# A graph network on one core: the place one-hots of the sort batches, and their products with the code, made in two halves of 64 places with a stop behind the first

## The chip, the core and the metric

The kernel runs on 1 core of one Trainium2 chip. The metric is the time on the device, in microseconds (us), of one execution; the number given for a kernel is the median of its runs. A profile is taken of one execution of its own, whose time stands beside the others.

## What is computed

Two graph layers over 3125 nodes of 128 features and 50,000 edges, the first a sum of neighbours with a small network behind it, the second a sum of messages whose weight depends on the edge's type (16 types, made of 8 bases):

```python
h = jnp.maximum(_layernorm(x, axis=-1), 0.0)
neigh = jax.ops.segment_sum(h[src], dst, num_segments=3125)
rst = (1.0 + eps[0]) * h + neigh
x = x + relu(relu(rst @ W1 + b1) @ W2 + b2)
h = jnp.maximum(_layernorm(x, axis=-1), 0.0)
weights = jnp.einsum('rb,bio->rio', coefficients, bases)
out = h @ w_self.T
msg = h[dst] @ weights[edge_type_16]      # per edge: one of 16 matrices
x = x + out.at[src].add(msg)
```

## The kernel before

**Sorting edges by matmul.** The edges are put into chunks of 128 that share a bucket of target nodes, so that a chunk's sum is a matrix product. There are four sorts, numbered 0 to 3: sorts 0, 1 and 2 take 72, 128 and 200 columns of 125 edges of the first layer and give 77, 131 and 208 chunks; sort 3 (`LAST`) takes all 400 columns of the second layer and gives 410 chunks. A sort places each edge's code at (place 0 to 127, chunk) in PSUM bank 7: VectorE makes a one-hot of the place and a one-hot of the chunk, one of the two is multiplied by the code, and TensorE multiplies them. Columns go in batches of 8 (`BATCH`), and the operands of a batch have two buffers (`BATCH_BUFS`). So sort 1 has 16 batches, sort 2 has 25 and sort 3 has 50.

**One batch of sort 3** (`sort_batch`): VectorE waits until TensorE has used the buffer (`batch_used`), makes the place one-hots of 8 columns in one instruction, `place_hot` of 125 x 1024 (L733), stops for it (`place_ready`), makes `place_val_a`, its product with the code's high part, in one instruction of the same size (L738), stops for it, and makes 8 chunk one-hots of 410 (L743). ScalarE starts at `place_ready` and makes 8 products with the code's low part, `place_val_b` (L498). TensorE then runs 16 products of 410 columns (L972, L974). **One batch of sorts 1 and 2** (`sort_pair`): one `place_hot` (L752), a stop, and 8 chunk one-hots already multiplied by the code's high part (L758); ScalarE adds the low part (L490); TensorE runs 8 products (L982).

**Gathering and adding up beside the next sort.** While sort s+1 is made, the chunks of sort s are added up (`groups_beside`): in groups of 4 chunks for the first layer, VectorE makes a `node_hot` for each chunk (L806), GpSimd gathers the chunk's 128 rows of the table `h_table` by an indirect DMA (L423), and TensorE multiplies the gathered rows by the node_hot (L1003, 3 products a chunk). Beside sort 3 run 47 of the 52 groups of sort 2; its last 5 come behind the decoding of sort 3 (`groups_rest`). Each engine has its own program, and the order within one is as written:

```python
for g in range(BESIDE[s + 1][1]):
    group_work(s, g)

    batches_alone(s + 1, sort_batch, *batches_after(s + 1, g))
```

**How far GpSimd may run ahead.** The first layer has 105 groups in all (20, 33 and 52, here numbered 0 to 104 across the three sorts), whose rows go round a ring of 13 groups. Before GpSimd gathers group g it waits until TensorE has used group g - lag:

```python
left = GROUPS_L[0] - gg if l == 0 else 2 * RING_L[1] - (gg - RING_L[1])
return min(RING_L[l], max(LEAST_LAG + l, left // 2))
```

The lag is 13 up to group 79, falls by one every two groups from there, and is 4 from group 96. Behind the first layer's last group come the dense part, the storing of the second layer's table and the gathers of the second layer. The helper `own` makes VectorE wait for the end of the instruction it was given, by semaphore `v`. Behind each `sort_batch` and `sort_pair` the same engine goes on with the next group's node_hots.

Of the kernel before, what the change touches and what calls it, by code (L numbers as in the profile page):

```python
# [9 lines left out]
ALU = mybir.AluOpType  # L10
# [4 lines left out]
P = 128  # L15
# [8 lines left out]
EP = N_EDGES // EC  # L24
# [33 lines left out]
BATCH = 8  # L58
# [21 lines left out]
def build(nc, x, src, dst, etype, eps, W1, b1, W2, b2, bases, coef, w_self, out):  # L80
    ctx = ExitStack()
    with ctx:
        def sb(name, shape, dt):
            return ctx.enter_context(nc.sbuf_tensor(name, shape, dt))
# [13 lines left out]
        iota_run = sb("iota_run", [P, P, BATCH], F16)  # L98
# [41 lines left out]
        place_h = [sb(f"place_h{l}", [EP, EC], F16) for l in range(2)]  # L140
        code_a = [sb(f"code_a{l}", [EP, EC], F16) for l in range(2)]
# [16 lines left out]
        place_hot = sb("place_hot", [EP, BATCH_BUFS, P, BATCH], F16)  # L158
        place_val_a = sb("place_val_a", [EP, BATCH_BUFS, P, BATCH], F16)
# [390 lines left out]
        def _(dve):  # L550
            done = 0

            def own(ins):

                nonlocal done
                ins.then_inc(v, 1)
                done += 1
                dve.wait_ge(v, done)

            V = nc.vector  # L560
# [167 lines left out]
            def sort_batch(s, batch, buf):  # L728

                l, c0, *_ = SORTS[s]  # L730
                dve.wait_ge(batch_used, batch + (BATCHES_BEFORE[s] + 1))
                run = slice(c0 + batch * BATCH, c0 + (batch + 1) * BATCH)
                V.tensor_tensor(place_hot[:, buf, :, :], iota_run[0:EP, :, :],  # L733
                                place_h[l][:, run].rearrange("p (o c) -> p o c", o=1).to_broadcast([EP, P, BATCH]),
                                ALU.is_equal).then_inc(place_ready, 1)
                done_before = batch + (BATCHES_BEFORE[s] - BATCHES_BEFORE[1] + 1)
                dve.wait_ge(place_ready, done_before)
                V.tensor_tensor(place_val_a[:, buf, :, :], place_hot[:, buf, :, :],  # L738
                                code_a[l][:, run].rearrange("p (o c) -> p o c", o=1).to_broadcast([EP, P, BATCH]),
                                ALU.mult).then_inc(val_a_ready, 1)  # L740
                dve.wait_ge(val_a_ready, batch + 1)
                for i in range(BATCH):
                    last = V.tensor_scalar(chunk_hot[:, buf, i, 0:CHUNKS[s]], iota_h[0:EP, 0:CHUNKS[s]],  # L743
                                           chunk_f[l][:, c0 + batch * BATCH + i:c0 + batch * BATCH + i + 1], None, ALU.is_equal)
                last.then_inc(batch_ready, 1)

            def sort_pair(s, batch, buf):

                l, c0, *_ = SORTS[s]
                dve.wait_ge(batch_used, batch + (BATCHES_BEFORE[s] + 1))  # L750
                run = slice(c0 + batch * BATCH, c0 + (batch + 1) * BATCH)
                V.tensor_tensor(place_hot[:, buf, :, :], iota_run[0:EP, :, :],  # L752
                                place_h[l][:, run].rearrange("p (o c) -> p o c", o=1).to_broadcast([EP, P, BATCH]),
                                ALU.is_equal).then_inc(place_ready, 1)
                dve.wait_ge(place_ready, batch + (BATCHES_BEFORE[s] - BATCHES_BEFORE[1] + 1))
                for i in range(BATCH):
                    c = c0 + batch * BATCH + i
                    V.tensor_scalar(pair_hot_of[s][:, buf, i, 0, :], iota_h[0:EP, 0:CHUNKS[s]], chunk_f[l][:, c:c + 1],  # L758
                                    code_f[:, c:c + 1], ALU.is_equal, ALU.mult).then_inc(pair_ready, 1)
# [99 lines left out]
            for s in range(1, NSORT):  # L859

                rank_place(s)
                if s > 1:

                    dve.wait_ge(nhot_used, CHUNKS_BEFORE[s - 1])
                groups_beside(s - 1, node_hots, sort_batch if s == LAST else sort_pair)
                if s == LAST:
                    read_sorted(s)
                else:
                    read_pair(s)
                decode(s)  # L870
                groups_rest(s - 1, node_hots)
                if s < LAST:
                    if s + 1 == LAST:
                        dve.wait_ge(w_stored, 32)
                    rank_count(s + 1)
# [248 lines left out]
```

## Time and profile before

| | |
|---|---|
| time, median of 3 runs | 1236.69 us (1233.98 to 1239.51) |
| time of the profiled execution | 1234.93 us |
| its span, first to last instruction | 1233.1 us |
| VectorE busy | 718.0 us (58%) |
| TensorE busy | 897.0 us (73%) |
| GpSimd busy | 834.9 us (68%) |
| ScalarE busy | 372.5 us (30%) |
| 416 gathers of the first layer, busy | 443.7 us |
| 410 gathers of the second layer, busy | 388.6 us |

The shares are means over stages that differ: sort 3 runs from about 409 to 616 us, the first layer's last product ends at 642 us, and the second layer's gathers fill the time from 772 us on. An engine's idle time matters only where another one waits for it, so the table is to be read with the rows of each stage. Times within the profile count from the start of the span.

### The profile page before, as it was taken

The numbers are of one execution on the slowest core, as the hardware profiler recorded it, in microseconds if no ns is written. First come the engines' busy times: TensorE is split into PE (matmuls) and PEld (weight loads), VectorE is DVE, ScalarE is ACT, GpSimd is POOL, SyncE is SP. The second block draws the span as 40 slices with busy tenths as digits, with TensorE's granted clock in tenths as the row PEclk, the third lists the DMA queues.
The fourth block names the chain that finished last, engine by engine and source line by source line (L and its number), as shares of the span: only waits on it lengthen the run. The fifth ranks groups of instructions, "written<-read, shape, count | busy, mean of one in ns | idle before, by whom it ended". The sixth has DMA issues, their size and how long they took to land.

```text
span 1233.1 us, 13150 instructions
## 1 busy us (share of the span) xinstructions
PE 897.0 (73%) x3799; PEld 571.9 (46%) x3799; DVE 718.0 (58%) x2165; ACT 372.5 (30%) x945; POOL 834.9 (68%) x833
## 2 busy tenths in 40 slices
PE   4777848978744899999959998965655655655654
PEld 2443424434312577777634433844444444444443
DVE  7896569857578899999935432833222323322331
ACT  7444314635300588888804432000000000000001
POOL 0177757778777777777740475777777777777772
PEclk9688878989986899999968999977777777677677
DMA  4443323433342334334333898212122122121224
GB/s 100 121 134 113 108 61 101 135 105 100 107 110 75 106 105 133 110 105 138 107 49 121 264 299 266 54 52 54 52 54 54 51 54 53 52 53 52 53 54 73
DMA packets 50307, 122.86 MB, mean 100 GB/s; under 512 B 16156, under 2 KB 27021, under 8 KB 47487
## 3 DMA queue, kind: packets, MB, share of 16 engines
q0 software_dynamic: 33088, 67.82, 21.8%
q1 hardware_dynamic: 16844, 52.62, 13.5%
q10 hardware_dynamic: 308, 1.60, 0.5%
q8 instruction: 34, 0.56, 0.2%
q14 instruction: 33, 0.27, 0.1%
HBM read 71.86 MB, written 50.10 MB: 99 GB/s over the span
## 4 chain that ended last, share of the span: by engine, by line
POOL 25%; issue 9%; PE 8%; SPq 4%; DVE 2%; DMA 2%; ACT 0%; POOLq 0%; DVEq 0%; ACTq 0%
POOL gathered L423 25%; SPq L382 4%; PE ps L999 3%; PE ps L1081 2%; DMA gathered<-z_table,row_of 1%; DVE spare L890 1%; PE ps L1058 1%; PE ps L1048 1%; PE ps L1095 0%; DMA z_table<-spare 0%; DMA gathered<-h_table,row_of 0%; PE ps L1003 0%; DVE x_sb L920 0%; ACT spare L519 0%; DVE stats L580 0%
## 5 line engine op out<-in xcount | busy, mean ns | idle before, releaser
L423 POOL DMA_INDIRECT gathered<-h_table,row_of x416 | 443.7, 1067 | 187.7 <-issue 120.1
L423 POOL DMA_INDIRECT gathered<-z_table,row_of x410 | 388.6, 948 | 190.4 <-issue 120.0
L999 PE MATMUL ps<-node_hot,gathered 128*128 128x250 f32 x820 | 279.7, 511 | 170.7 <-DMA gathered<-z_table,row_of 170.7
L806 DVE TENSOR_SCALAR node_hot<-iota_f,key_of 128x250 f32<-128x250 f32 x410 | 153.8, 379 | 294.3 <-PE ps L999 286.1
L999 PEld LDWEIGHTS ps<-node_hot,gathered 128*128 128x128 f32 x820 | 208.1, 262 | 242.1 <-issue 207.0
L1003 PE MATMUL ps<-node_hot,gathered 128*128 128x506 bf16 (+1 forms) x1248 | 243.8, 350 | 75.9 <-DMA gathered<-h_table,row_of 57.6
L1003 PEld LDWEIGHTS ps<-node_hot,gathered 128*128 128x128 bf16 x1248 | 126.5, 103 | 179.4 <-issue 112.1
L498 ACT ACTIVATE place_val_b<-place_hot,code_b 125x128 f16<-125x128 f16 x400 | 173.8, 520 | 100.5 <-DVE place_hot L733 100.3
L490 ACT ACTIVATE scratch<-scratch,code_b 125x208 f16<-125x208 f16 (+1 forms) x328 | 114.4, 430 | 177.3 <-DVE scratch L758 177.3
L545 ACT COPY spare<-ps 128x500 f32<-128x500 f32 (+1 forms) x7 | 3.1, 563 | 459.8 <-PE ps L999 459.8
L972 PE MATMUL ps<-scratch,place_val_a 125*128 125x410 f16 x400 | 138.3, 346 | 2.6 <-DVE scratch L743 2.4
L974 PE MATMUL ps<-scratch,place_val_b 125*128 125x410 f16 x400 | 134.9, 337 | 0.0
L806 DVE TENSOR_SCALAR node_hot<-iota_h,key_of 128x506 bf16<-128x506 f16 (+1 forms) x416 | 107.5, 323 | 28.9 <-PE ps L1003 28.4
L743 DVE TENSOR_SCALAR scratch<-iota_h,chunk_f 125x410 f16<-125x410 f16 x400 | 102.6, 331 | 1.8
L1081 PE MATMUL ps<-w_rel,spare 128*125 128x512 f32 x200 | 90.7, 601 | 4.1 <-DVE spare L890 2.3
L758 DVE TENSOR_SCALAR scratch<-iota_h,chunk_f,spot_i 125x208 f16<-125x208 f16 (+1 forms) x328 | 83.7, 350 | 1.5
L972 PEld LDWEIGHTS ps<-scratch,place_val_a 125*128 125x128 f16 x400 | 57.6, 144 | 37.5 <-DVE scratch L743 6.7
L890 DVE COPY spare<-ps 125x1024 f32<-125x1024 f32 x25 | 30.5, 1221 | 60.1 <-PE ps L1081 32.4
L1081 PEld LDWEIGHTS ps<-w_rel,spare 128*125 128x125 f32 x200 | 35.5, 187 | 55.4 <-issue 31.7
L982 PE MATMUL ps<-scratch,place_hot 125*128 125x416 f16 (+1 forms) x328 | 57.1, 316 | 0.0
L982 PEld LDWEIGHTS ps<-scratch,place_hot 125*128 125x128 f16 x328 | 44.7, 145 | 14.0 <-issue 2.2
L752 DVE TENSOR_TENSOR place_hot<-iota_run,place_h 125x1024 f16<-125x1024 f16 x41 | 28.3, 689 | 39.1 <-PE ps L982 38.7
(170 smaller groups left out, 541.8 us busy)
## 6 DMA issues: line engine op xcount, KB each, us to landing
z_table<-spare SPq DMA_DIRECT2D x50, 448.0 KB
z_table<-zeros_z SPq DMA_DIRECT2D x19, 896.0 KB
gathered<-h_table,row_of POOLq DMA_INDIRECT x416
gathered<-z_table,row_of POOLq DMA_INDIRECT x410, 2.5
z_table<-spare SPq DMA_DIRECT2D x50, 52.0 KB
z_table<-zeros_z SPq DMA_DIRECT2D x19, 104.0 KB
out<-x_sb SPq DMA_DIRECT2D x6, 224.0 KB
h_table<-gathered SPq DMA_DIRECT2D x1, 1092.0 KB
```

The lines of the kernel that those rows point to most:

```text
L423: pool.indirect_dma_start(place if s == LAST else place.rearrange("p j d -> p (j d)"), None, z_table if s == LAST else h_table, bass.Indir ...
L490: nc.scalar.activation(pair_hot_of[s][:, buf, i, 1, :], pair_hot_of[s][:, buf, i, 0, :], ACT.Copy, scale=code_b[l][:, c0 + batch * BATCH + ...
L498: nc.scalar.activation(place_val_b[:, buf, i, :], place_hot[:, buf, :, i], ACT.Copy, scale=code_b[l][:, c0 + batch * BATCH + i:c0 + batch ...
L743: last = V.tensor_scalar(chunk_hot[:, buf, i, 0:CHUNKS[s]], iota_h[0:EP, 0:CHUNKS[s]], chunk_f[l][:, c0 + batch * BATCH + i:c0 + batch * B ...
L758: V.tensor_scalar(pair_hot_of[s][:, buf, i, 0, :], iota_h[0:EP, 0:CHUNKS[s]], chunk_f[l][:, c:c + 1], code_f[:, c:c + 1], ALU.is_equal, AL ...
L806: V.tensor_scalar(node_hot_of[s][:, k % HOTS[s], :], (iota_f if s == LAST else iota_h)[:, 0:WIDE[s]], key_of[s][:, k:k + 1], None, ALU.is_ ...
L972: T.matmul(ps[:, 7, 0:w], place_val_a[:, buf, :, i], hot, start=False, stop=False, skip_group_check=True)
L974: last = T.matmul(ps[:, 7, 0:w], place_val_b[:, buf, i, :], hot, start=False, stop=False, skip_group_check=True)
L982: last = T.matmul(ps[:, 7, 0:2 * CHUNKS[s]].rearrange("p (k w) -> p k w", k=2), place_hot[:, buf, :, i], pair_hot_of[s][:, buf, i, :, :], ...
L999: last = T.matmul(psf[:, bass.ds(offs[i], WIDE[s])], rows, node_hot_of[s][:, k % HOTS[s], :], start=False, stop=False, skip_group_check=True)
L1003: last = T.matmul(psf[:, bass.ds(offs[i], WIDE[s])], rows[:, part, :], node_hot_of[s][:, k % HOTS[s], :], start=False, stop=False, skip_gr ...
L1081: last = T.matmul(z_half(half)[:, q * BANK:(q + 1) * BANK], h2T[:, t * NP:(t + 1) * NP], w_rel[:, half * N_REL // 2 + q * BT:half * N_REL ...
```

## The change

In `sort_batch` and `sort_pair` the instruction that makes the place one-hots is made in two of 64 places, 125 x 512 each, and VectorE waits for the first before it issues the second; in `sort_batch` the same is done with their product with the code. What is computed is the same. Sort 0 (`sort_first`) is as before, and no other engine's program changes.

```diff
                 run = slice(c0 + batch * BATCH, c0 + (batch + 1) * BATCH)
-                V.tensor_tensor(place_hot[:, buf, :, :], iota_run[0:EP, :, :],
-                                place_h[l][:, run].rearrange("p (o c) -> p o c", o=1).to_broadcast([EP, P, BATCH]),
+                half = P // 2
+                places = place_h[l][:, run].rearrange("p (o c) -> p o c", o=1).to_broadcast([EP, half, BATCH])
+                own(V.tensor_tensor(place_hot[:, buf, 0:half, :], iota_run[0:EP, 0:half, :], places, ALU.is_equal))
+                V.tensor_tensor(place_hot[:, buf, half:P, :], iota_run[0:EP, half:P, :], places,
                                 ALU.is_equal).then_inc(place_ready, 1)
                 done_before = batch + (BATCHES_BEFORE[s] - BATCHES_BEFORE[1] + 1)
                 dve.wait_ge(place_ready, done_before)
-                V.tensor_tensor(place_val_a[:, buf, :, :], place_hot[:, buf, :, :],
-                                code_a[l][:, run].rearrange("p (o c) -> p o c", o=1).to_broadcast([EP, P, BATCH]),
+                codes = code_a[l][:, run].rearrange("p (o c) -> p o c", o=1).to_broadcast([EP, half, BATCH])
+                own(V.tensor_tensor(place_val_a[:, buf, 0:half, :], place_hot[:, buf, 0:half, :], codes, ALU.mult))
+                V.tensor_tensor(place_val_a[:, buf, half:P, :], place_hot[:, buf, half:P, :], codes,
                                 ALU.mult).then_inc(val_a_ready, 1)
                 dve.wait_ge(val_a_ready, batch + 1)
...
```

The second hunk makes the same edit to `place_hot` in `sort_pair`.

On VectorE, in the middle of sort 3, one batch and the group behind it stood like this before (`scratch` holds the chunk one-hots there):

```order
L733 TENSOR_TENSOR place_hot<-iota_run,place_h 125x1024 [waits batch_used]
L738 TENSOR_TENSOR place_val_a<-place_hot,code_a 125x1024 [waits place_ready]
L743 TENSOR_SCALAR scratch<-iota_h,chunk_f 125x410 [waits val_a_ready]
L743 TENSOR_SCALAR scratch<-iota_h,chunk_f 125x410 x7
L806 TENSOR_SCALAR node_hot<-iota_h,key_of 128x250 x4
```

At the same place of VectorE's program there now stand:

```order
L735 TENSOR_TENSOR place_hot<-iota_run,place_h 125x512 [waits batch_used]
L736 TENSOR_TENSOR place_hot<-iota_run,place_h 125x512 [waits v]
L741 TENSOR_TENSOR place_val_a<-place_hot,code_a 125x512 [waits place_ready]
L742 TENSOR_TENSOR place_val_a<-place_hot,code_a 125x512 [waits v]
L746 TENSOR_SCALAR scratch<-iota_h,chunk_f 125x410 [waits val_a_ready]
L746 TENSOR_SCALAR scratch<-iota_h,chunk_f 125x410 x7
L811 TENSOR_SCALAR node_hot<-iota_h,key_of 128x250 x4
```

Nothing changed places; two instructions and two waits for VectorE's own semaphore came in, and the lines below are numbered 3 or 5 higher.

On VectorE, in the middle of sort 2, a batch and its group stood like this before (`scratch` holds the chunk one-hots times the code):

```order
L752 TENSOR_TENSOR place_hot<-iota_run,place_h 125x1024 [waits batch_used]
L758 TENSOR_SCALAR scratch<-iota_h,chunk_f,spot_i 125x208 [waits place_ready]
L758 TENSOR_SCALAR scratch<-iota_h,chunk_f,spot_i 125x208 x7
L806 TENSOR_SCALAR node_hot<-iota_h,key_of 128x506 [waits nhot_used] x4
L752 TENSOR_TENSOR place_hot<-iota_run,place_h 125x1024 [waits batch_used]
```

and stand now:

```order
L757 TENSOR_TENSOR place_hot<-iota_run,place_h 125x512 [waits batch_used]
L758 TENSOR_TENSOR place_hot<-iota_run,place_h 125x512 [waits v]
L763 TENSOR_SCALAR scratch<-iota_h,chunk_f,spot_i 125x208 [waits place_ready]
L763 TENSOR_SCALAR scratch<-iota_h,chunk_f,spot_i 125x208 x7
L811 TENSOR_SCALAR node_hot<-iota_h,key_of 128x506 [waits nhot_used] x8
```

Here one instruction and one wait came in a batch.

## Rows read from the trace of the kernel before

**Rows 1.** Busy time by stage: us, busy (count) by engine, TensorE's clock, DMA share, GB/s

```profile
409.00:470.00 61.00, 59.56 (x385) 42.63 (x386) 59.99 (x201) 48.91 (x113) 47.84 (x44) 0.94 0.42 121
470.00:530.00 60.00, 59.61 (x401) 43.03 (x398) 58.99 (x202) 51.23 (x119) 46.89 (x44) 1.00 0.38 106
530.00:616.00 86.00, 85.06 (x568) 61.23 (x566) 84.29 (x287) 73.34 (x170) 67.11 (x63) 1.00 0.42 120
```

**Rows 2.** Groups by shape, 409 to 616 us: count | busy us, mean ns | idle before

```profile
L423 POOL DMA_INDIRECT gathered<-h_table,row_of x149 | 162.7, 1092 | 45.4 <-issue 41.8 <-PE ps L1003 3.7
L743 DVE TENSOR_SCALAR scratch<-iota_h,chunk_f 125x410 f16<-125x410 f16 x400 | 102.6, 331 | 1.8
L738 DVE TENSOR_TENSOR place_val_a<-place_hot,code_a 125x1024 f16<-125x1024 f16 x50 | 34.6, 692 | 1.7
L733 DVE TENSOR_TENSOR place_hot<-iota_run,place_h 125x1024 f16<-125x1024 f16 x50 | 33.9, 679 | 0.0
```

**Rows 3.** Timeline of VectorE in sort 3: start us, us

```profile
480.90 0.68 DVE L733 TENSOR_TENSOR place_hot<-iota_run,place_h 125x1024 f16<-125x1024 f16 x1
481.62 0.69 DVE L738 TENSOR_TENSOR place_val_a<-place_hot,code_a 125x1024 f16<-125x1024 f16 x1
482.35 1.99 DVE L743 TENSOR_SCALAR scratch<-iota_h,chunk_f 125x410 f16<-125x410 f16 x8
485.02 0.68 DVE L733 TENSOR_TENSOR place_hot<-iota_run,place_h 125x1024 f16<-125x1024 f16 x1
```

**Rows 4.** Timeline of TensorE in sort 3: first and last product of a batch, a group

```profile
484.40 0.39 PE L972 MATMUL ps<-scratch,place_val_a 125*128 125x410 f16 x1
487.07 0.33 PE L974 MATMUL ps<-scratch,place_val_b 125*128 125x410 f16 x1
487.24 1.45 PE L1003 MATMUL ps<-node_hot,gathered 128*128 128x250 bf16 x12
```

**Rows 5.** Timeline of VectorE in sort 0, whose instructions stand close

```profile
29.08 0.69 DVE L723 TENSOR_TENSOR place_hot<-iota_run,place_h 125x1024 f16<-125x1024 f16 x1 [0.26 <-PE ps L962]
29.69 0.47 DVE L724 TENSOR_TENSOR scratch<-iota_run,chunk_h 125x616 f16<-125x616 f16 x1
30.59 0.47 DVE L726 TENSOR_TENSOR scratch<-scratch,first_b 125x616 f16<-125x616 f16 x1
30.98 0.22 DVE L824 RECIPROCAL rstd<-sd 125x12 f32<-125x12 f32 x1
```

**Rows 6.** Waits of the whole span: us in total, times, longest

```profile
DVE place_hot L752 <- PE ps L982: 38.7, 16, 6.3
PE ps L1003 <- DMA gathered<-h_table,row_of: 57.6, 22, 5.5
```

**Rows 7.** Timeline of GpSimd: a gather beside L738, one alone, one beside L733

```profile
469.85 1.42 POOL L423 DMA_INDIRECT gathered<-h_table,row_of  x1 [0.30 <-issue]
471.57 0.95 POOL L423 DMA_INDIRECT gathered<-h_table,row_of  x1 [0.30 <-issue]
481.33 1.08 POOL L423 DMA_INDIRECT gathered<-h_table,row_of  x1 [0.30 <-issue]
```

**Rows 8.** Timeline: TensorE's use of group 92, GpSimd's first gather of group 96

```profile
581.65 1.45 PE L1003 MATMUL ps<-node_hot,gathered 128*128 128x250 bf16 x12
586.73 1.10 POOL L423 DMA_INDIRECT gathered<-h_table,row_of  x1 [0.30 <-PE ps L1003]
```

**Rows 9.** Timeline of the end of the first layer

```profile
622.27 6.66 PE L1003 MATMUL ps<-node_hot,gathered 128*128 128x250 bf16 x36 [3.45 <-DVE node_hot L806]
629.98 0.95 POOL L423 DMA_INDIRECT gathered<-h_table,row_of  x1 [0.30 <-issue]
633.73 0.95 POOL L423 DMA_INDIRECT gathered<-h_table,row_of  x1 [0.30 <-issue]
639.51 2.68 PE L1003 MATMUL ps<-node_hot,gathered 128*128 128x250 bf16 x12 [4.17 <-DMA gathered<-h_table,row_of]
642.22 3.02 DVE L881 COPY scratch<-ps 128x500 f32<-128x500 f32 x5 [16.60 <-PE ps L1003]
```

More of the change, by code:

```diff
@@ L751, in sort_pair @@
                 run = slice(c0 + batch * BATCH, c0 + (batch + 1) * BATCH)
-                V.tensor_tensor(place_hot[:, buf, :, :], iota_run[0:EP, :, :],
-                                place_h[l][:, run].rearrange("p (o c) -> p o c", o=1).to_broadcast([EP, P, BATCH]),
+                half = P // 2
+                places = place_h[l][:, run].rearrange("p (o c) -> p o c", o=1).to_broadcast([EP, half, BATCH])
+                own(V.tensor_tensor(place_hot[:, buf, 0:half, :], iota_run[0:EP, 0:half, :], places, ALU.is_equal))
+                V.tensor_tensor(place_hot[:, buf, half:P, :], iota_run[0:EP, half:P, :], places,
                                 ALU.is_equal).then_inc(place_ready, 1)
```

## The prediction

> **What bounds the kernel now.** I read the busy time by stage first. From 409 to 616 us, while sort 3 is made, VectorE is busy for 203.3 of 207 us and TensorE for 204.2 [rows 1], so the mean of 58% for VectorE over the span says nothing about this stretch. The reader should see that three engines are full there at once: GpSimd too, since 149 gathers of 1.092 us with 0.30 us between them make 207 us [rows 2, 7]. So the question is which of the three has to wait for another.
>
> The groups of that stage answer for VectorE. Before `place_hot`, the instruction that waits for TensorE to free a buffer, VectorE sat idle for 0.0 us in 50 batches, and before the other two kinds for 1.7 and 1.8 us in all [rows 2]. It never waits, so sort 3 runs at VectorE's pace. The timeline gives that pace: from one `place_hot` to the next 485.02 - 480.90 = 4.12 us, group of node_hots included [rows 3]. TensorE needs almost as much: 487.24 - 484.40 = 2.84 us for the 16 products and at most 1.45 us for the group's 12, so at most 4.29 us and by its timeline about 4.1 [rows 4].
>
> GpSimd needs 4 x (1.092 + 0.30) = 5.6 us for a group of four, more than the 4.12 us in which a group is used. It starts the stage with up to 13 groups gathered and lives on them. By group 96 it has 586.73 - (581.65 + 1.45) = 3.6 us between TensorE's use of group 92 and its own start [rows 8]. At the end it is late: TensorE waits 4.17 us for the last group's rows, and the first layer's sums are copied out at 642.22 us [rows 9]. So the end of the first layer is set by GpSimd by a small margin, with VectorE right behind it.
>
> In sorts 1 and 2 it is otherwise: VectorE waits 38.7 us for TensorE before `place_hot`, and TensorE waits 57.6 us for gathers of the first layer [rows 6]. There GpSimd sets the pace and VectorE has time to spare.
>
> **The cost of one split.** Without a stop, VectorE's next instruction starts 29.69 - 29.08 = 0.61 us behind a place one-hot of 1024, and 30.98 - 30.59 = 0.39 us behind one of 616 [rows 5]. That is 0.22 us for 408 elements, 0.54 ns each, so 512 elements are worth 0.275 us and the rest of an instruction is about 0.06 us. With a stop the same 1024 take 0.72 and 0.73 us from start to start [rows 3]. A half with a stop is then 0.725 - 0.275 = 0.45 us, two halves 0.90, and a split costs 0.175 us; since these rows are rounded to 0.01 us I take 0.18. It can't be under 0.06, which an instruction costs with no stop at all. From above, the smallest instruction here with a stop behind it bounds it: the reciprocal of 12 elements takes 0.22 us [rows 5], so with a gap of 0.03 us at most 0.25.
>
> **Where it is hidden.** Sorts 1 and 2 have 16 + 25 = 41 splits, 7.4 us of VectorE. They lie in the 38.7 us in which VectorE waits for TensorE before just this instruction [rows 6], so I cost them at nothing; without that cover they would cost the 7.4 us.
>
> **Where it is not.** Sort 3 has 50 batches with two splits each: 100 x 0.18 = 18.0 us, on an engine with no idle time in that stage. The period with a group goes from 4.12 to 4.48 us, and TensorE's 4.1 to 4.29 us still fits, so VectorE stays the bound. Behind the waiting instruction stand the chunk one-hots and the next group's node_hots, for which TensorE waits, and TensorE's use of a group is what GpSimd waits for. ScalarE gets its place one-hots 0.18 us later in each batch; its 8 products take 48.91 + 51.23 + 73.34 = 173.5 of the 207 us [rows 1], so it is no new bound.
>
> **What comes back to GpSimd.** A gather beside the two long instructions took 1.42 us, one beside a place one-hot 1.08 us, one alone 0.95 us [rows 7]. So these VectorE instructions hold a gather up, and halves with a stop between them should hold it up less. Before sort 3 this counts, because GpSimd sets the pace there: with 41 place one-hots, a stretch of 0.13 us and half of it saved, at most 2.7 us, at least nothing, since not each meets a gather. I take 1.5 us: sort 3 starts that much earlier. In sort 3 what GpSimd gains turns into waiting. The use of group 92 comes 42 batches into the sort, so 42 x 0.36 - 1.5 = 13.6 us later, and the 3.6 us [rows 8] are used up: GpSimd must wait for it, and group 96 starts at about 597 instead of 586.7 us.
>
> The Trainium skill, "SBUF — State Buffer", section "Who interferes with whom", says that a tensor_tensor with both inputs in SBUF takes only the read side of the port pair that VectorE and GpSimd share, and infers that generating a DMA's descriptors is not held up by it. The 1.42 us of rows 7 speak against the inference. By the page the 1.5 us would not come back and the sum would be 12 instead of 10.5 us.
>
> **The end of the layer.** The sorted columns are ready for the last five groups 18.0 - 1.5 = 16.5 us later. Group 100 is the first of the 36 products that start at 622.27 us and take 6.66 us [rows 9]; it is used by about 624.9 us, as the first of the three at the lowered clock. GpSimd's gathers of group 104, the last, start at 629.98 us [rows 9] and need group 100 used: 5.1 us to spare. So they start 16.5 - 5.1 = 11.4 us later. Then 4 gathers of 1.25 us, the landing, and 2.68 us of products as before. The landing was slow: the last issue ended at 634.68 and TensorE began at 639.51 us, 4.8 us later [rows 9]. With group 103 issued before and then a pause, less stands in the DMA queues, which may give back between 0 and 3 us. I take 0.9.
>
> **Sum.** +18.0 - 1.5 - 5.1 - 0.9 = +10.5 us at the copy that stood at 642.22 us. What follows is unchanged and moves with it. The profiled execution took 1234.9 us (span 1233.1), 1.8 us under the median of 1236.7; against that median the changed kernel comes to 1247 us, 0.85% slower.
>
> **Rivals.**
>
> *Slower, by the page* (chance 0.05): GpSimd's descriptors are not held up by these instructions, and nothing comes back before sort 3: 1248.7 us. The row of 1.42 us is against it.
>
> *A stop costs little, or the end absorbs more* (0.15): at a split of 0.06 to 0.12 us, 100 splits are 6 to 12 us, and after 1.5 and 5.1 us of slack -0.6 to +5.4 are left; about 1239 us, no measurable change. For it: VectorE's start-to-start times are read from rounded rows. Against it: 0.72 against 0.61 us for the same 1024 elements is what a stop adds, 0.11 us, and the fixed 0.06 stands beside it.
>
> *Faster: GpSimd keeps the pace* (0.07). In sort 3, gathers lose 149 x (1.092 - 0.95) = 21 us [rows 2, 7]. If the halves return some 8 us of it and VectorE's added time stays within the slack, the last group is gathered that much earlier: 1229 us. It decides where a split costs VectorE under 0.05 us, so that 100 of them stay under the 5.1 us at the end. For it speaks that TensorE waits for gathers 57.6 us in all [rows 6]; against it, that VectorE has no idle time in just this stage.
>
> *Much slower: TensorE loses its full clock* (0.08). The granted clock in sort 3 was 0.94, 1.00 and 1.00 with TensorE busy 98% and more [rows 1]; the changed kernel has it wait some 0.2 to 0.4 us in each batch. Below a mean of 4.12 / 4.48 = 0.92 TensorE would be slower than VectorE; at 0.85 a batch takes 4.85 us, 0.37 us more, 18 us in all: 1265 us.
>
> **How the numbers follow.** The forecast has the remaining 0.65. Its own range is a split of 0.15 to 0.21 us (15 to 21 us), 0 to 2.7 us back, and 0 to 3 us at the landing: +4 to +16, with the ends rarely together, so 1242 to 1253. For 8 in 10 I add the flat case and part of the slow one: 1238 to 1258. The measurement can tell about 0.5%, 6.2 us. Faster is 0.07, within it is 0.15, and slower is the forecast, the page's case and the clock's: 0.78.
>
> **What would show it.** Right: in the profile after, the halves last about 0.42 us each, 100 of each kind of `place_hot` and `place_val_a` in sort 3; that stage's period is near 4.48 us; VectorE still has no idle time in it; a gather of the first layer is under 1.067 us in the mean; GpSimd's waits on `nhot_used` appear as gaps of several us from about group 90 on; the copy of 642.22 us stands near 653. Wrong: a period near 4.2, or TensorE at a granted clock under 0.95 between 415 and 630 us, or GpSimd without gaps.

## The result, and the profile after

| | before | after |
|---|---|---|
| time, median of 3 runs | 1236.69 us | 1247.64 us (1245.78 to 1248.31) |
| time of the profiled execution | 1234.93 us | 1245.78 us |
| its span | 1233.1 us | 1244.0 us |

The ratio is 1.0085, with a 95% interval of [1.0045, 1.0125]: the change made the kernel slower by 5.6 to 15.5 us. All comparisons in this document are of fast runs: one execution, of e6_after_lag13, took 2062 us and is left out.

The busy time of the changed kernel by stage, to be read against [rows 1] (us, busy and count of TensorE, its weight loads, VectorE, ScalarE, GpSimd, then TensorE's clock, DMA share, GB/s):

```profile
407.00:468.00 61.00, 56.82 (x359) 39.48 (x358) 59.13 (x211) 45.81 (x106) 46.98 (x47) 0.94 0.41 118
468.00:528.00 60.00, 55.55 (x361) 38.88 (x360) 58.16 (x209) 46.04 (x108) 41.66 (x43) 1.00 0.40 114
528.00:630.00 102.00, 93.77 (x612) 65.77 (x610) 98.95 (x351) 76.64 (x178) 61.00 (x63) 1.00 0.35 100
```

VectorE is busy for nearly as large a share as before, 97% after 98%; TensorE no longer: 206.1 of 223 us instead of 204.2 of 207. GpSimd fell too. TensorE's clock did not: 0.94, 1.00 and 1.00, as before. So one engine is full where three were.

The groups of sort 3 of the changed kernel, for [rows 2]:

```profile
L423 POOL DMA_INDIRECT gathered<-h_table,row_of x154 | 153.4, 996 | 74.6 <-issue 43.3 <-PE ps L1008 31.3
L977 PE MATMUL ps<-scratch,place_val_a 125*128 125x410 f16 x392 | 136.0, 347 | 17.2 <-DVE scratch L746 17.2
L746 DVE TENSOR_SCALAR scratch<-iota_h,chunk_f 125x410 f16<-125x410 f16 x399 | 104.7, 336 | 1.8
L742 DVE TENSOR_TENSOR place_val_a<-place_hot,code_a 125x512 f16<-125x512 f16 x50 | 21.3, 425 | 1.7
L736 DVE TENSOR_TENSOR place_hot<-iota_run,place_h 125x512 f16<-125x512 f16 x50 | 21.2, 425 | 1.7
L735 DVE TENSOR_TENSOR place_hot<-iota_run,place_h 125x512 f16<-125x512 f16 x49 | 20.2, 412 | 0.0
```

Four things are to be seen. A half lasts 412 to 425 ns, where the whole lasted 679 and 692: two halves are 0.15 us more, before the stop. VectorE still has no idle time before the instruction that waits for TensorE (L735). TensorE now waits 17.2 us for chunk one-hots. And GpSimd, whose gathers became shorter (996 instead of 1092 ns), now spends 31.3 us waiting for TensorE.

The timeline of VectorE in one batch, for [rows 3]:

```profile
483.74 0.41 DVE L735 TENSOR_TENSOR place_hot<-iota_run,place_h 125x512 f16<-125x512 f16 x1
484.19 0.42 DVE L736 TENSOR_TENSOR place_hot<-iota_run,place_h 125x512 f16<-125x512 f16 x1
484.65 0.42 DVE L741 TENSOR_TENSOR place_val_a<-place_hot,code_a 125x512 f16<-125x512 f16 x1
485.11 0.43 DVE L742 TENSOR_TENSOR place_val_a<-place_hot,code_a 125x512 f16<-125x512 f16 x1
485.57 2.13 DVE L746 TENSOR_SCALAR scratch<-iota_h,chunk_f 125x410 f16<-125x410 f16 x8
488.39 0.41 DVE L735 TENSOR_TENSOR place_hot<-iota_run,place_h 125x512 f16<-125x512 f16 x1
```

From the first half to the chunk one-hots are 485.57 - 483.74 = 1.83 us; before they were 482.35 - 480.90 = 1.45 [rows 3]. That is 0.38 us a batch, 0.19 a split. The period of this batch is 4.65 us instead of 4.12; the other 0.15 us lie in its chunk one-hots (2.13 us, where [rows 3] have 1.99) and behind. Over all 50 batches the mean is 228.1 / 50 = 4.56 us instead of 206.3 / 50 = 4.13.

GpSimd's timeline, where it now waits (for [rows 8]: the waits of 4 us have taken the place of the time to spare):

```profile
593.35 0.95 POOL L423 DMA_INDIRECT gathered<-h_table,row_of  x1 [0.30 <-issue]
598.27 0.97 POOL L423 DMA_INDIRECT gathered<-h_table,row_of  x1 [3.98 <-PE ps L1008]
```

The end of the first layer, for [rows 9]:

```profile
640.31 4.07 DVE L811 TENSOR_SCALAR node_hot<-iota_h,key_of 128x250 bf16<-128x250 f16 x20
640.83 5.31 PE L1008 MATMUL ps<-node_hot,gathered 128*128 128x250 bf16 x48 [3.25 <-DVE node_hot L811]
642.56 1.06 POOL L423 DMA_INDIRECT gathered<-h_table,row_of  x1 [3.13 <-PE ps L1008]
646.43 0.95 POOL L423 DMA_INDIRECT gathered<-h_table,row_of  x1 [0.30 <-issue]
651.33 2.68 PE L1008 MATMUL ps<-node_hot,gathered 128*128 128x250 bf16 x12 [5.18 <-DMA gathered<-h_table,row_of]
654.05 3.80 DVE L886 COPY scratch<-ps 128x500 f32<-128x500 f32 x7 [9.67 <-PE ps L1008]
```

The last gathers start as soon as TensorE has used group 100, after a wait of 3.13 us; before, they started without one. The copy of the sums moved from 642.22 to 654.05 us, by 11.8, and the span by 10.9.

### The profile page after: what moved, and what is told of

Same layout as the page of the kernel before. It is cut to its first block, busy times and chain, and to the rows that moved or that the text cites. A ratio compares the mean times of both kernels' runs of the same rounds, so it can differ in the third digit from the quotient of the medians.

```text
span 1244.0 us, 13291 instructions
## 1 busy us (share of the span) xinstructions
PE 899.7 (72%) x3799; PEld 571.6 (46%) x3799; DVE 741.2 (60%) x2306; ACT 371.5 (30%) x945; POOL 817.6 (66%) x833
## 3 DMA queue, kind: packets, MB, share of 16 engines
q0 software_dynamic: 33088, 67.82, 21.4%
## 4 chain that ended last, share of the span: by engine, by line
POOL 24%; DVE 22%; PE 10%; issue 9%; SPq 3%; DMA 3%; ACT 0%; POOLq 0%; DVEq 0%; ACTq 0%
POOL gathered L423 24%; DVE scratch L746 8%; PE ps L1004 4%; DVE node_hot L811 3%; SPq L382 3%; PE ps L1086 2%; DVE place_val_a L742 2%; DVE place_hot L736 2%; DVE place_val_a L741 2%; DVE spare L632 1%; DMA gathered<-z_table,row_of 1%; PE ps L957 1%; DVE place_hot L735 1%; DVE spare L895 1%; DMA z_table<-spare 1%
## 5 line engine op out<-in xcount | busy, mean ns | idle before, releaser
L423 POOL DMA_INDIRECT gathered<-h_table,row_of x416 | 427.2, 1027 | 217.0 <-issue 120.7
L1004 PE MATMUL ps<-node_hot,gathered 128*128 128x250 f32 x820 | 282.7, 515 | 167.6 <-DMA gathered<-z_table,row_of 167.6
L1008 PE MATMUL ps<-node_hot,gathered 128*128 128x506 bf16 (+1 forms) x1248 | 238.0, 344 | 73.2 <-DMA gathered<-h_table,row_of 55.3
L895 DVE COPY spare<-ps 125x1024 f32<-125x1024 f32 x25 | 30.5, 1221 | 61.2 <-DMA z_table<-spare 32.8
L979 PEld LDWEIGHTS ps<-scratch,place_val_b 125*128 125x128 f16 x400 | 40.8, 102 | 10.8 <-issue 0.5
```

What stands on the lines that cost most here:

```text
L423: pool.indirect_dma_start(place if s == LAST else place.rearrange("p j d -> p (j d)"), None, z_table if s == LAST else h_table, bass.Indir ...
L979: last = T.matmul(ps[:, 7, 0:w], place_val_b[:, buf, i, :], hot, start=False, stop=False, skip_group_check=True)
L1004: last = T.matmul(psf[:, bass.ds(offs[i], WIDE[s])], rows, node_hot_of[s][:, k % HOTS[s], :], start=False, stop=False, skip_group_check=True)
L1008: last = T.matmul(psf[:, bass.ds(offs[i], WIDE[s])], rows[:, part, :], node_hot_of[s][:, k % HOTS[s], :], start=False, stop=False, skip_gr ...
```

## The experiments

For each kernel two things are given: its ratio to the kernel before with the 95% interval, from 6 to 12 runs (3 for the change itself), and what its one profile shows. The times in us are worked out from the ratio. Executions of one and the same kernel differ by up to 10 us to either side of the median, and in the profiles most of that lies before sort 3. So sort 3 and what follows it in the first layer are read apart. "Sort 3" runs from the start of its first place one-hot to the end of its last chunk one-hot, "tail" from there to the start of the copy of the sums, both from VectorE's timeline; the two together ("both" in the table) are called the stage. "Stall" is the time by which the gathers issued in sort 3 exceed 0.945 us each, "waits" the time by which GpSimd's gaps between gathers exceed 0.305 us from sort 3 to the end of the layer.

| kernel | splits in sort 3 | ratio, 95% | sort 3 | tail | both | stall | waits |
|---|---|---|---|---|---|---|---|
| before | 0 | 1 | 206.3 | 26.5 | 232.8 | 21.9 | 0.0 |
| the change | 100 | 1.0085 [1.0045, 1.0125] | 228.1 | 19.5 | 247.6 | 7.9 | 30.5 |
| e1_pair_only | 0 | 0.9994 [0.9966, 1.0022] | 204.9 | 28.6 | 233.5 | 22.1 | 0.0 |
| e2_batch_only | 100 | 1.0112 [1.0071, 1.0152] | 228.1 | 18.5 | 246.6 | 8.2 | 29.7 |
| e3_no_stop | 100, no stop | 1.0054 [1.0027, 1.0081] | 216.7 | 21.4 | 238.1 | 23.1 | 3.9 |
| e4_quarters | 300 | 1.0443 [1.0401, 1.0485] | 268.4 | 20.6 | 289.0 | 7.4 | 73.2 |
| e5_hot_only | 50 | 1.0012 [0.9980, 1.0043] | 217.6 | 20.4 | 238.0 | 6.4 | 20.7 |
| e6_after_lag13 | 100 | 1.0004 [0.9980, 1.0027] | 226.3 | 14.6 | 240.9 | 9.7 | 0.0 |
| e7_before_lag13 | 0 | 0.9993 [0.9971, 1.0015] | 206.2 | 27.3 | 233.5 | 22.1 | 0.0 |
| e8_pair_lag13 | 0 | 0.9949 [0.9922, 0.9976] | 204.9 | 27.9 | 232.8 | 21.1 | 0.0 |
| e9_half2_lag13 | 25 | 0.9921 [0.9890, 0.9952] | 211.4 | 14.6 | 226.0 | 11.7 | 0.0 |
| e10_half4_lag13 | 13 | 0.9917 [0.9883, 0.9951] | 209.4 | 18.7 | 228.1 | 17.6 | 0.0 |
| e11_hot_lag13 | 50 | 0.9955 [0.9925, 0.9986] | 217.0 | 14.4 | 231.4 | 8.0 | 0.0 |
| e12_pairq_lag13 | 0 | 0.9978 [0.9949, 1.0007] | 205.7 | 27.1 | 232.8 | 21.8 | 0.0 |

For the stage a single profile stands for a kernel. In the five kernels whose sort 3 is that of the kernel before, it took 204.9 to 206.3 us, and 232.8 to 233.5 together with the tail.

My theory, A: in sort 3 each split costs VectorE a fixed time that nothing hides, and the end of the layer takes off what time GpSimd's lateness had left there, once. Against it stood B, that GpSimd's waits are what costs, and that the cost is not one per split.

### Each part alone: e1_pair_only and e2_batch_only

The first halves only in sorts 1 and 2, the second only in sort 3. The edit that `sort_pair` keeps in the first:

```diff
-                V.tensor_tensor(place_hot[:, buf, :, :], iota_run[0:EP, :, :],
-                                place_h[l][:, run].rearrange("p (o c) -> p o c", o=1).to_broadcast([EP, P, BATCH]),
+                own(V.tensor_tensor(place_hot[:, buf, 0:half, :], iota_run[0:EP, 0:half, :], places, ALU.is_equal))
+                V.tensor_tensor(place_hot[:, buf, half:P, :], iota_run[0:EP, half:P, :], places,
                                 ALU.is_equal).then_inc(place_ready, 1)
```

> Only the place one-hots of sorts 1 and 2 are halved (41 splits), sort 3 is as before. Theory A (the loss is VectorE's fixed cost in sort 3; in sorts 1 and 2 it is hidden, and the gathers gain there): 2 to 3 us faster than before, since sort 3 started 3.0 us earlier in the changed kernel and GpSimd ends the layer. Theory B (the relief of the gathers is worth nothing): within 1 us of before.

Measured: 0.7 us faster, between 4.2 faster and 2.7 slower. No change can be told from it; A's 2 to 3 us and B's 1 us are both inside, and both theories stand.

> Only sort 3's place one-hots and products are halved (100 splits). Theory A: the whole loss without the gain, 13 to 15 us slower than before. If the 3 us at the start of sort 3 come from elsewhere: 11 us slower, as the full change.

Measured: 13.9 us slower (8.8 to 18.8), in the range that A gave, though the interval holds 11 too. Sort 3 is 228.1 us long, exactly as with the full change, so the loss sits in sort 3.

### The stop or the instruction: e3_no_stop

```diff
-                own(V.tensor_tensor(place_hot[:, buf, 0:half, :], iota_run[0:EP, 0:half, :], places, ALU.is_equal))
+                V.tensor_tensor(place_hot[:, buf, 0:half, :], iota_run[0:EP, 0:half, :], places, ALU.is_equal)
```

The same for `place_val_a`, and in `sort_pair`.

> Halves as in the change, but with no stop behind the first. Theory A: an instruction costs about 0.08 us without a stop, so sort 3 grows by 8 us instead of 21.7, and with 5 to 6 us to spare at the end the kernel is 0 to 3 us slower than before: 0 if the gathers get in between two halves without a stop too, 3 if they get in only at a stop. Rival, the cost of a split is in the instruction and not in the stop: 8 to 11 us slower.

Measured: 6.7 us slower (3.3 to 10.0), which is in neither range. The timeline of VectorE in this kernel:

```profile
482.66 0.41 DVE L735 TENSOR_TENSOR place_hot<-iota_run,place_h 125x512 f16<-125x512 f16 x1
482.99 0.41 DVE L736 TENSOR_TENSOR place_hot<-iota_run,place_h 125x512 f16<-125x512 f16 x1
483.44 0.47 DVE L741 TENSOR_TENSOR place_val_a<-place_hot,code_a 125x512 f16<-125x512 f16 x1
```

The second half starts 0.33 us behind the first, where it was 0.45 with a stop; so of 0.19 us a split, the stop is 0.12 and the instruction 0.07. Sort 3 grew by 10.4 us, 7 of them from 100 splits: the cost of an instruction is as A had it. Most of the rest is in the chunk one-hots, which I had not counted. The gathers are the second finding. In this kernel they last as long as before in the mean:

```profile
L423 POOL DMA_INDIRECT gathered<-h_table,row_of x147 | 160.7, 1093 | 48.7 <-issue 41.7 <-PE ps L1008 7.0
```

1093 ns in the mean against 1092 [rows 2] and 996 in the changed kernel. Halves alone give GpSimd nothing; with the stop they do. The last section shows why.

### The dose: e4_quarters and e5_hot_only

Quarters of 32 places, each but the last with a stop behind it; and halves of the place one-hots alone in sort 3, 50 splits instead of 100.

```diff
-                half = P // 2
+                half = P // 4
...
-                own(V.tensor_tensor(place_hot[:, buf, 0:half, :], iota_run[0:EP, 0:half, :], places, ALU.is_equal))
-                V.tensor_tensor(place_hot[:, buf, half:P, :], iota_run[0:EP, half:P, :], places,
+                for q in range(3):
+                    part = slice(q * half, (q + 1) * half)
+                    own(V.tensor_tensor(place_hot[:, buf, part, :], iota_run[0:EP, part, :], places, ALU.is_equal))
+                V.tensor_tensor(place_hot[:, buf, 3 * half:P, :], iota_run[0:EP, 3 * half:P, :], places,
                                 ALU.is_equal).then_inc(place_ready, 1)
```

> Quarters of 32 places in place of halves, with a stop behind each: three times the splits. Theory A: sort 3 grows by 3 x 19.3 = 58 us, and of this 3 to 5 us come back before it and 6 at the end: 45 to 50 us slower than before, about 1284 us. Rival, the loss is a wait that comes once (a lost overlap with GpSimd) and not per split: 11 to 20 us slower.

Measured: 54.8 us slower (49.6 to 60.0). That is above my range, with its end just inside the interval, and it rules out a loss that comes once. Sort 3 grew by 62.1 us, the tail shrank by 5.9.

> In sort 3 only the place one-hots are halved, their product with the code is as before; sorts 1 and 2 as in the change. Theory A with the time to spare at the end (5 to 6 us) taken off once: sort 3 grows by 10 to 11 us, starts 3 us earlier, and the kernel is 1 to 3 us slower than before. Rival, half the splits cost half of what the change cost: 5.5 us slower.

Measured: 1.5 us slower (2.5 faster to 5.3 slower). By the times alone the rival's 5.5 is only just outside. The profile is clearer: sort 3 and the tail together are 5.2 us longer, 11.3 in sort 3 and 6.1 off the tail; with the full change they are 14.8 longer. Half the splits cost a third, not half.

Together the doses give one line: 11.3 us for 50 splits, 21.8 for 100, 62.1 for 300, that is 0.23, 0.22 and 0.21 us each. Counted from start to start, the place one-hots and their products alone took 72.0 us in the kernel before, 91.3 in the changed one and 129.7 with quarters, which is 0.19 us a split at both doses. And the tail gives back 6.1, 7.0 and 5.9 us, once.

### How far GpSimd may run ahead: e6_after_lag13 and e7_before_lag13

```diff
-            return min(RING_L[l], max(LEAST_LAG + l, left // 2))
+            return RING_L[0] if l == 0 else min(RING_L[l], max(LEAST_LAG + l, left // 2))
```

> The changed kernel, in which GpSimd may gather 13 groups ahead to the end of the first layer. Theory A: VectorE's node_hots for the last five groups still come at 640 us, but the last gathers no longer wait, and TensorE does the five groups in a row in 6.7 us: the layer ends at 647.5 instead of 654 us, 6.5 us faster than the change, 4.5 us slower than before. Theory B (it is GpSimd's waits that cost, not VectorE): the loss is gone, within 1 us of before.

Measured: 0.5 us slower than before (2.5 faster to 3.3 slower). By the time that is B's number, and below my 4.5. But the profile doesn't bear B out. Sort 3 is still 20.0 us longer than before, and it and the tail together 8.1 us. The end of the layer in this kernel:

```profile
613.94 1.07 POOL L423 DMA_INDIRECT gathered<-h_table,row_of  x1 [0.30 <-issue]
634.83 3.99 DVE L811 TENSOR_SCALAR node_hot<-iota_h,key_of 128x250 bf16<-128x250 f16 x20
635.35 8.26 PE L1008 MATMUL ps<-node_hot,gathered 128*128 128x250 bf16 x60 [3.25 <-DVE node_hot L811]
643.65 3.02 DVE L886 COPY scratch<-ps 128x500 f32<-128x500 f32 x5 [4.83 <-PE ps L1008]
```

GpSimd issues its last gather at 613.94 us, 21 us before the node_hots for which its rows are meant, and the five groups run in one piece. The layer ends when VectorE lets it. Against the changed kernel, sort 3 and the tail are 6.7 us shorter, about the 6.5 I expected. By the runs it is 10 us faster than the changed kernel, 3 to 4 more than the stage accounts for; the lag differs only from group 80 on, which is gathered in sort 3, and why stays open. What the stretch ahead of sort 3 is worth in all these kernels is taken up below.

> The kernel before with the same 13 groups ahead to the end. Both theories: GpSimd never waited for this in the kernel before, so within 1 us of it.

Measured: 0.9 us faster (3.6 faster to 1.9 slower), as both said.

### Whether the cover in sorts 1 and 2 holds: e8_pair_lag13 and e12_pairq_lag13

The first is e1_pair_only with the lag of 13, the second has quarters in `sort_pair` in place of halves.

> Halves in sorts 1 and 2 only, and 13 groups ahead to the end. Theory A: 2 to 3 us faster than before, as with the halves alone, since GpSimd doesn't wait in sort 3 there. If the earlier gathers run into the shrinking lag: up to 1 us better than without it.

Measured: 6.3 us faster (9.6 to 3.0). It differs from e1_pair_only only in a wait that never came into play in either, so the two are best read together: their intervals meet at 3 to 4 us faster, a little above the 2 to 3 us of A. Sort 3 and the tail are 232.8 us, as before; what is gained lies ahead of sort 3.

> Sorts 1 and 2 in quarters with stops (123 splits, 23 us of VectorE), sort 3 as before, 13 groups ahead. Theory A: VectorE's idle time of 35 to 39 us before these instructions still covers it: 2 to 4 us faster than before, as with halves. If the cover is used up in the stretches where VectorE has no idle time: 2 to 8 us slower.

Measured: 2.7 us faster (6.3 faster to 0.9 slower). VectorE's waits for TensorE, and TensorE's for gathers, in this kernel:

```profile
PE ps L1007 <- DMA gathered<-h_table,row_of: 57.7, 27, 5.1
DVE place_hot L756 <- PE ps L986: 34.5, 12, 6.8
DVE node_hot L810 <- PE ps L1007: 17.0, 8, 4.1
DVE scratch L770 <- PE ps L986: 8.8, 2, 5.3
```

The same waits in the kernel before, beside the 38.7 us of [rows 6]:

```profile
DVE node_hot L806 <- PE ps L1003: 28.4, 15, 5.0
DVE scratch L766 <- PE ps L982: 15.3, 2, 8.2
```

With 23 us of splits in sorts 1 and 2 the kernel isn't slower: the cover holds at three times the dose. But it is not the cover that the prediction named. The wait before the place one-hot fell only from 38.7 to 34.5 us; the three kinds of wait together fell from 82.4 to 60.3, by 22.1, and most of that came out of the waits before the node_hots and at the end of a sort.

### Fewer splits: e9_half2_lag13, e10_half4_lag13 and e11_hot_lag13

If a split costs VectorE 0.22 us and returns time to GpSimd, then the best number is where both paths to the end of the layer are equal. In sort 3, of the place one-hots only every second batch (25 splits), every fourth (13) or each (50) is halved; `place_val_a` is whole:

```diff
+                if batch % 2 == 0:
+                    half = P // 2
+                    places = place_h[l][:, run].rearrange("p (o c) -> p o c", o=1).to_broadcast([EP, half, BATCH])
+                    own(V.tensor_tensor(place_hot[:, buf, 0:half, :], iota_run[0:EP, 0:half, :], places, ALU.is_equal))
+                    V.tensor_tensor(place_hot[:, buf, half:P, :], iota_run[0:EP, half:P, :], places,
+                                    ALU.is_equal).then_inc(place_ready, 1)
+                else:
```

> In sort 3 only the place one-hots of every second batch are halved (25 splits); sorts 1 and 2 halved as in the change; 13 groups ahead to the end. Theory A: the layer ends with the later of two paths. VectorE: sort 3 grows by 25 x 0.22 = 5.5 us to 211.8, and 14.6 us follow. GpSimd: its stalls in sort 3, 21.9 us before and 6.4 with a split in each batch, fall by half of that. Both then end 6.4 to 7.5 us sooner than before, and 2 us come from sorts 1 and 2: 8 us faster than before, 1229. Theory P (the stalls fall only where the batches' period as a whole falls out of step with the gathers): nothing is gained in sort 3, 0 to 2 us faster than before.

Measured: 9.8 us faster (13.6 to 5.9). Sort 3 and the tail are 226.0 us, 6.8 shorter than before, as worked out. The groups of 407 to 616 us show the two sides:

```profile
L423 POOL DMA_INDIRECT gathered<-h_table,row_of x159 | 161.9, 1018 | 48.4 <-issue 44.5 <-PE ps L1012 4.0
L740 DVE TENSOR_TENSOR place_hot<-iota_run,place_h 125x1024 f16<-125x1024 f16 x25 | 17.0, 680 | 0.0
L737 DVE TENSOR_TENSOR place_hot<-iota_run,place_h 125x512 f16<-125x512 f16 x24 | 10.3, 427 | 0.8
```

Gathers are down to 1018 ns, and GpSimd's last one starts at 617.87 us, just ahead of the node_hots at 621.29: here the two paths to the end of the layer meet.

> The same with every fourth batch (13 splits). Theory A: VectorE adds 2.9 us, GpSimd's stalls fall by a quarter of 15.5, 3.9 us, and the layer is GpSimd's: 4 to 6 us faster than before. Theory P: 0 to 2 us faster.

Measured: 10.3 us faster (14.5 to 6.1), more than A's 4 to 6. The stage is 4.7 us shorter than before; the times can't tell it from e9.

> The same with every batch (50 splits). Theory A: VectorE's path is 217.6 + 14.6 = 232.2 us against 232.8 before, so nothing is left but what sorts 1 and 2 give: 1 to 3 us faster than before, and GpSimd has its last gather done well over 5 us before TensorE wants it. If what VectorE pays is not what bounds it: 8 us faster or more.

Measured: 5.6 us faster (9.3 to 1.7), above A's 1 to 3, though the interval reaches there. The stage is 1.4 us shorter. From 25 to 50 splits sort 3 grows by 5.6 us and the tail stays at 14.4 to 14.6: all that is added is VectorE's.

All three beat both the kernel before and the changed one, with the same edit at a half, a quarter or an eighth of its dose in sort 3 and the lag of 13. Not all of that comes from sort 3: e8_pair_lag13, with no split there, is 6.3 us faster too, and against it alone neither e9 nor e10 is clear of noise. The mean ratio of e9 and e10 is 0.9919, that of e1 and e8, which differ from them by the splits in sort 3 (and e1 by the lag, worth nothing there by e7), 0.9972. That is 6.5 us, give or take some 4 (an estimate from the four intervals), and the stages are 6.8 and 4.7 us shorter. Theory P, that nothing is gained in sort 3 at such a dose, is out by this. That e9 and e10 are better than e11, with 50 splits, rests on the stage of one profile each: 226.0 and 228.1 us against 231.4.

## Why the prediction was right

The direction, the place and the time came out as forecast: 1247.6 us measured, 1247 predicted, and 11.8 us at the copy of the sums, where 10.5 were worked out. The terms behind it were less exact than the sum.

**The cost of one split.** Taken at 0.18 us; 0.19 in the timeline of VectorE, 0.21 to 0.23 when sort 3's growth is divided by the splits. The 0.19 is the two fixed parts, 0.07 for an instruction and 0.12 for a stop. The rest is a cost that I left out: the 400 chunk one-hots lasted 336 instead of 331 ns in the mean, 2 us in all. Why they did stays open. It is not the number of splits alone: in e6_after_lag13, with the same 100 splits and more gathers in sort 3 (162 instead of 154), they lasted 332 ns.

**Sort 3's growth.** 18.0 us was worked out, 21.8 measured: 19.3 in the split instructions and 2.5 in the chunk one-hots and the gaps between them. This is the term that was mis-sized.

**What comes back before sort 3.** Taken at 1.5 us. Sort 3 began 3.0 us earlier in the profile after, but the profiles of all kernels spread over more than that: from the first gather to sort 3 they take 346.0 to 356.3 us with stopped halves or quarters in sorts 1 and 2 and 351.9 to 357.5 without. In the runs, e1, e8 and e12 give 0.7, 6.3 and 2.7 us, and the changed kernel against e2_batch_only gives 2.7 us less. If from each kernel's measured difference the difference of its stage (the column "both") is taken off, the ten kernels with stopped halves or quarters in sorts 1 and 2 are 1.4 to 7.6 us faster in the rest, 4.0 in the mean; the three without are 1.6 faster, 0.1 slower and 1.4 slower. So the gain is there, and nearer to 4 us than to the 1.5 taken.

The spread of the profiles has a cause that they show themselves. The stretch from the first gather to sort 3 is the longer, the more its 253 to 255 gathers exceed 0.945 us each: 346.0 us at 22.4 us of such stall (e6), 351.9 at 28.4 (before), 357.5 at 34.9 (e7), and the other eleven lie along the same line. The stall is 26.5 us in the mean of the ten with stopped parts and 32.0 in that of the four without. That it also makes most of the difference between executions of one and the same kernel would fit, but each kernel has one profile.

**The cover in sorts 1 and 2.** Costing 41 splits at nothing was right, but they did not all come out of the 38.7 us before the place one-hot: in the changed kernel that wait is still 34.4 us, and e12_pairq_lag13 shows that the other waits of VectorE cover the most.

**GpSimd must wait.** Forecast from about group 90 on, group 96 at about 597 us; it starts there at 598.27 us, after a wait of 3.98. Waits of 31.3 us in sort 3 appeared. The first came earlier than said, before group 84 at 510.7 us: the gathers had become shorter than I allowed for.

**The end of the layer.** 5.1 + 0.9 = 6.0 us were to be absorbed; the tail became 7.0 us shorter. The last group's gathers started 12.6 us later than before; 11.4 was worked out. The landing gave back what was taken: from the end of the last gather to TensorE's start 4.0 us instead of 4.8. e6_after_lag13 shows what this was made of: of the 26.5 us in the tail before, 14.6 are VectorE's and TensorE's own, and 12 were a wait for GpSimd. With the lag of 4 groups about 5 of these 12 stay when VectorE is late; without it none do. So "by a small margin" was wrong: GpSimd was 12 us late, and only the lag kept the time to spare down to 5.1.

**The rivals.** That a stop costs little is out (e3_no_stop: 0.12 us of 0.19). That GpSimd keeps the pace is out for the change, by its waits of 31.3 us. Its condition, a split under 0.05 us, was too strict: at 0.19 us a split e9 and e10 are faster, with fewer splits and the lag of 13. That TensorE loses its clock did not happen; it was 1.00 with TensorE busy 92% of the time. As to the page of the Trainium skill, "SBUF — State Buffer", section "Who interferes with whom": its inference that a tensor_tensor does not hold up the generation of descriptors is not borne out here. Only the tensor_tensor instructions of VectorE were edited, and the gathers' mean went from 1092 to 996 ns with halves and stops, and not at all with halves that run into each other (1093). The same section says that such a tensor_tensor does contend with a GpSimd instruction that reads SBUF; whether a gather is held up where it reads its row numbers, no run here shows.

**Errors that met.** By the two profiles the growth was taken 3.8 us too small, and so was what comes off it: 1.0 us too little at the tail, 1.5 ahead of sort 3, and 0.9 in the rest of the kernel behind the layer's end. They nearly cancel; that the sum agrees to 1 us is luck.

## What to carry to other kernels

When several engines are all full in a stage, ask which one never waits: there, each added instruction and each stop costs its fixed time in full, and could here be priced to some 20% from two start-to-start rows of different size. An edit that trades time of that engine for time of another has a best dose: work out both paths to the stage's end and stop where they meet. Here that was at 13 to 25 splits of the 100 tried, once GpSimd might run 13 groups ahead; by the stage in the profile, while the times alone only separate these two doses together from none. The time to spare at a stage's end is given back once, whatever the dose: 5 to 8 us in the kernels with the lag of 4, from 50 splits to 300.

## What the runs showed of the hardware

A gather's issue on GpSimd took 0.95 us when nothing held it up, 1.42 us beside one of these VectorE instructions [rows 7], and 1.70 us at most in sort 3. The row of 0.95 us is not one where VectorE rested, as "alone" may be read: the chunk one-hots ran beside it.

```profile
469.76 0.69 DVE L738 TENSOR_TENSOR place_val_a<-place_hot,code_a 125x1024 f16<-125x1024 f16 x1
470.49 2.12 DVE L743 TENSOR_SCALAR scratch<-iota_h,chunk_f 125x410 f16<-125x410 f16 x8
```

The gather of 469.85 us ended 0.82 us behind the end of L738, in the midst of chunk one-hots, and the one of 471.57 ran beside chunk one-hots in 0.95 us. So the long hold-ups come from the long two-input instructions. Small ones come beside the chunk one-hots too: 33 gathers issued 1.8 us into a batch, with chunk one-hots alone beside them, took 1.03 us in the mean.

What a half is worth is best seen at one and the same place, where a gather is issued 0.01 to 0.02 us behind the first place one-hot of a batch. The kernel before:

```profile
505.90 0.68 DVE L733 TENSOR_TENSOR place_hot<-iota_run,place_h 125x1024 f16<-125x1024 f16 x1
505.91 1.49 POOL L423 DMA_INDIRECT gathered<-h_table,row_of  x1 [0.30 <-issue]
```

Halves with no stop (e3_no_stop), where the second starts before the first has ended:

```profile
479.08 0.41 DVE L735 TENSOR_TENSOR place_hot<-iota_run,place_h 125x512 f16<-125x512 f16 x1
479.09 1.55 POOL L423 DMA_INDIRECT gathered<-h_table,row_of  x1 [0.30 <-issue]
479.41 0.41 DVE L736 TENSOR_TENSOR place_hot<-iota_run,place_h 125x512 f16<-125x512 f16 x1
```

The changed kernel, with the first half at 483.74 us:

```profile
483.76 1.22 POOL L423 DMA_INDIRECT gathered<-h_table,row_of  x1 [0.30 <-issue]
```

In each case the gather ends 0.81 to 0.83 us behind the end of what VectorE was at when it began: the whole instruction, both halves that run into each other, or the first half alone. The lengths repeat: in sort 3, 17 gathers at this place lasted 1.48 to 1.49 us with the instruction whole (before, e1, e7, e8), 34 lasted 1.54 to 1.56 with halves and no stop (e3), and 47 lasted 1.21 to 1.23 with halves and the stop (the change, e2, e6). Cutting the instruction in two freed GpSimd only when VectorE stopped between the parts: a stall of 23.1 us over sort 3 without the stop, 7.9 us with it, 21.9 uncut.

I had expected that halves would save half of the stall at most. At the same place they did just that: 0.27 of the 0.54 us over 0.945. Over the whole sort they saved two thirds (21.9 to 7.9 us), and halving only one of the two instructions saved as much (6.4). So the rest must come from where in the batch the gathers fall. In the kernel before, three gathers of 1.03 to 1.10 us fit the period of 4.12 us and met VectorE at the same places in one batch after another:

```profile
495.09 1.03 POOL L423 DMA_INDIRECT gathered<-h_table,row_of  x1 [0.30 <-issue]
496.43 1.10 POOL L423 DMA_INDIRECT gathered<-h_table,row_of  x1 [0.30 <-issue]
497.83 1.08 POOL L423 DMA_INDIRECT gathered<-h_table,row_of  x1 [0.30 <-issue]
499.22 1.03 POOL L423 DMA_INDIRECT gathered<-h_table,row_of  x1 [0.30 <-issue]
```

In all 50 batches of that sort a gather of 1 us or more was under way as the chunk one-hots started, in the changed kernel in 21. There most gathers take 0.95 us, with a period of 4.64 us in the median. That the longer period broke a lock between the two engines would fit. A longer period by itself does not bring the relief: with 4.33 us a batch in the mean e3_no_stop has a stall of 23.1 us, and e5_hot_only, with 4.35, one of 6.4. But no run changed the period alone, so how much of the relief is the halves' and how much the rhythm's stays open beyond that one place.
